# Attention's queries, keys and maxima as two float32r parts of 12 bits, in a 32-row tile for each head

## The reference

```python
def _L0_attn_ref(x, wq, bq, wk, bk, wv, bv, wo, bo):
    ...
    q = split(x @ wq.T + bq); k = split(x @ wk.T + bk); v = split(x @ wv.T + bv)
    scale = Dh ** 0.5
    scores = jnp.einsum('bhsd,bhtd->bhst', q, k) / scale
    scores = jnp.where(causal, scores, -jnp.inf)
    weights = jax.nn.softmax(scores, axis=-1)
    ctx = jnp.einsum('bhst,bhtd->bhsd', weights, v)
    return ctx.transpose(0, 2, 1, 3).reshape(B, S, E) @ wo.T + bo

x = x + 0.5 * _L0_ffn_ref(_layernorm(x), ...)     # 8 experts, top 2, capacity 1.25
x = x + _L0_attn_ref(_layernorm(x), ...)
x = x + 0.5 * _L0_ffn_ref(_layernorm(x), ...)
```

## Time and profile before

| | |
|---|---|
| median of 3 runs | 1033.29 us (1031.57 to 1038.26) |
| span of the profiled execution | 1036.6 us |
| PE busy | 831.8 us (80%) |
| DVE busy | 601.5 us (58%) |
| ACT busy | 523.4 us (50%) |
| POOL busy | 489.6 us (47%) |
| mean granted clock of PE | 0.890 |

### The profile page before, as it was taken

The page is one execution under the profiler, slowest core; times in us unless marked ns, Lnnn a source line. Parts: engine busy times, 40 slices in busy tenths (PEclk is TensorE's granted clock), DMA queues, the critical chain, the costliest instruction groups (busy, mean ns, idle before and its releaser), DMA issues. The chain is left out here.

```text
span 1036.6 us, 18080 instructions
## 1 busy us (share of the span) xinstructions
PE 831.8 (80%) x6599; PEld 446.5 (43%) x6599; DVE 601.5 (58%) x1237; ACT 523.4 (50%) x841; POOL 489.6 (47%) x686
## 2 busy tenths in 40 slices
PE   8569999944668988888978899878887618999990
PEld 7437878742212223332333323323232316787770
DVE  7931211124767788888787977878775423334235
ACT  6323343442237776777556786566766303433330
POOL 5047455325652662646467522562224651545453
PEclk9769999986657999999799999999899758999995
DMA  7115575621451262341524224323202124423236
GB/s 204 73 26 153 148 217 145 192 63 51 130 162 66 53 189 48 89 144 43 174 76 105 99 53 152 85 65 106 53 18 79 53 63 149 130 79 97 78 136 228
DMA packets 96185, 110.81 MB, mean 107 GB/s; under 512 B 12279, under 2 KB 68763, under 8 KB 96104
## 3 DMA queue, kind: packets, MB, share of 16 engines
q1 hardware_dynamic: 84752, 88.86, 29.1%
q0 software_dynamic: 9216, 17.98, 6.8%
q10 hardware_dynamic: 2136, 2.91, 0.8%
HBM read 57.86 MB, written 52.89 MB: 107 GB/s over the span
## 5 line engine op out<-in xcount | busy, mean ns | idle before, releaser
L1903 DVE TENSOR_REDUCE m_blk<-banks 128x8 f32<-128x1024 f32 (+1 forms) x320 | 348.5, 1114 | 79.7 <-PE banks L1505 67.1
L1823 ACT ACTIVATE pt<-banks 128x1024 f32<-128x1024 f32 (+3 forms) x384 | 300.4, 811 | 145.1 <-PE banks L1489 142.7
L1537 PE MATMUL banks<-pt,vs 128*32 128x512 f32 (+3 forms) x1536 | 176.6, 534 | 7.2 <-POOL pt L2252 3.8
L1489 PE MATMUL banks<-qb,kp 64*128 64x512 bf16 (+3 forms) x768 | 132.6, 351 | 53.7 <-DVE m_blk L1903 45.2
L2252 POOL TENSOR_SCALAR_AFFINE_SELECT pt<-pt 128x512 f32<-128x512 f32 x128 | 81.6, 637 | 192.1 <-ACT pt L1823 191.7
L1505 PE MATMUL banks<-kp,qa 64*128 64x128 bf16 (+4 forms) x1152 | 126.4, 294 | 19.6 <-ACT pt L1823 11.6
L849 POOL DMA_INDIRECT xe<-xn_rows,slot_tok x80 | 79.9, 999 | 94.4 <-PE banks L1190 37.2
L675 POOL DMA_INDIRECT y_tab<-ys,ids x70 | 68.0, 972 | 81.5 <-DVE ys L635 64.5
L1106 ACT ACTIVATE he<-banks,b_up 128x512 f32<-128x512 f32 (+1 forms) x96 | 57.9, 616 | 89.9 <-PE banks L1190 89.5
L1505 PEld LDWEIGHTS banks<-kp,qa 48*128 48x128 bf16 (+1 forms) x1152 | 46.2, 99 | 130.3 <-ACT pt L1823 92.7
L585 ACT ACTIVATE hT<-banks,bfc 128x512 f32<-128x512 f32 (+1 forms) x96 | 56.3, 615 | 84.9 <-DVE bfc L607 48.8
(11 more groups left out here) (344 smaller groups left out, 1128.8 us busy)
## 6 DMA issues: line engine op xcount, KB each, us to landing
bucket<-zero SPq DMA_DIRECT2D x16, 660.0 KB
qb<-q_stack SPq DMA_DIRECT2D x32, 192.0 KB, 3.5
qa<-q_stack SPq DMA_DIRECT2D x30, 192.0 KB, 3.3
kp<-k_stack SPq DMA_DIRECT2D x30, 192.0 KB, 4.2
q_stack<-qp SPq DMA_DIRECT2D x18, 256.0 KB
k_stack<-kq SPq DMA_DIRECT2D x18, 256.0 KB
y_slots<-ye SPq DMA_DIRECT2D x16, 256.0 KB, 2.5
mid<-x SPq DMA_DIRECT2D x8, 512.0 KB, 3.6
```

The costliest lines, as they stand in the source:

```text
L1489: i = nc.tensor.matmul(ring[SLOT["score", 2 * u + pair]][:, s, 0:w], kp[g][rows_s, pair, kb * P:(kb + 1) * P], qb[par][rows_s, pair, q0:q0 ...
L1537: i = nc.tensor.matmul(o_bank[VW * h:VW * h + VW, q:q + w], vs[par][:, kb, h, :], pt[u % PTS][:, h, 0:w], start=u in (0, SECOND), stop=u i ...
L1823: nc.scalar.activation(pt[u % PTS][:, 2 * pair:2 * pair + 2, 0:w], ring[SLOT["score", 2 * u + pair]][:, :, 0:w], ACT.Exp, scale=SCALE).the ...
L1903: nc.vector.tensor_reduce(dst, ring[slot][:, :, 0:blocks * P].rearrange("p s (j k) -> p s j k", k=P), AX.X, ALU.max).then_inc(m_done, 1)
```

## The change

Queries and keys become two float32r parts instead of three bf16 parts. float32r is a float32 whose writer rounds it to 12 bits of mantissa, so that a matmul takes it as a single operand; part 1 is what part 0 leaves. The products kept are part 0 by part 0, part 0 by part 1 and part 1 by part 0: three slots of 8 rows, 24 in all, plus 2 rows for the maximum and 4 for the diagonal. A head now has a tile of 32 rows, and the four heads of a group lie in the four quarters of the 128 partitions; `qa`, `qb` and `kp` lose the axis of pairs and hold 4 bytes per value, so their size is the same.

- `score` and `maxima`: as many matmuls of the same widths as before, on 32 rows (24 where the diagonal isn't marked) of float32r instead of 64 (48) of bf16. Pair 0 is in partitions 0 to 63, pair 1 in 64 to 127.
- ACT: `second_part` goes, 16 copies of 128x512; `stack_take` is 4 copies instead of 8. DVE and POOL: `third_part` goes (4 on DVE, 12 on POOL); DVE's `remainder` writes part 1 itself.
- POOL: `split_max` has 2 steps instead of 5, since the sign is now in `k_edge`. The constants take 20 selects on 32 rows in place of 10 on 64, and 6 copies in place of 12.
- PE in the prologue: `stack_parts` makes 12 matmuls instead of 32. The transpose of the maxima is float32 on 32 columns instead of bf16 on 48.
- DMA: three pieces for queries and three for keys in place of six and six, of the same total bytes; a load of a stack is four DMAs of 24 rows instead of two of 48 by 2; the maxima come back in four DMAs instead of two.

The diff, cut to its core:

```diff
-    Q_PART = [0, 0, 0, 1, 1, 2]
-    K_PART = [0, 1, 2, 0, 1, 0]
+    Q_PART = [0, 0, 1]
+    K_PART = [0, 1, 0]
+    HR = 32
     KS = len(Q_PART) * DH
     EDGE, STEP = KS + 4, 32
...
-            qa = [sba(f"qa{i}", [P, HS // 2, S], bf16) for i in range(2)]
-            qb = [sba(f"qb{i}", [P, HS // 2, S], bf16) for i in range(2)]
-            kp = [sba(f"kp{i}", [P, HS // 2, S], bf16) for i in range(NG)]
+            qa = [sba(f"qa{i}", [P, S], f32r) for i in range(2)]
+            qb = [sba(f"qb{i}", [P, S], f32r) for i in range(2)]
+            kp = [sba(f"kp{i}", [P, S], f32r) for i in range(NG)]
...
-            parts = [[sba(f"{n}{j}", [P, S], bf16) for j in range(3)] for n in ("qp", "kq")]
-            rest = sba("rest", [P, 2, 512])
+            parts = [[sba(f"{n}{j}", [P, S], f32r) for j in range(2)] for n in ("qp", "kq")]
...
-            m_neg = sba("m_neg", [P, HS, T // 2])
-            m_parts = [sba(f"m_parts{i}", [P, 3, HS, T // 2], bf16) for i in range(2)]
-            MR = 3 * HS * T // 2
-            m_rows = [sba(f"m_rows{i}", [MR, P], bf16) for i in range(2)]
+            m_parts = [sba(f"m_parts{i}", [P, 2, HS, T // 2], f32r) for i in range(2)]
+            MR = 2 * HS * T // 2
+            m_rows = [sba(f"m_rows{i}", [MR, P]) for i in range(2)]
...
-                for j in range(3):
-                    eng.wait_ge((part_one, rest_ok, split_ok)[j], 3 + which)
+                for j in range(2):
+                    if j == 0:
+                        eng.wait_ge(part_one, 3 + which)
+                    else:
+                        eng.wait_ge(c_evac, pro_at[("q1", "k1")[which]] + 1)
                     for c in range(len(order)):
                         if order[c] == j:
                             dst = stack[0:NH * KS, :].rearrange("(h c d) n -> c h d n", h=NH, d=DH)[c]
-                            eng.dma_start(dst[h0:h1], parts[which][j][h0 * DH:h1 * DH, :]).then_inc(done, 16)
+                            eng.dma_start(dst[h0:h1], parts[which][j][h0 * DH:h1 * DH, :].bitcast(f32)).then_inc(done, 16)
...
-                    src = stack[bass.ds(b * NH * KS + g * HS * KS, HS * KS), :].rearrange("(i s r) n -> s r i n", s=2, r=KS)
-                    for s in range(2):
-                        sp.dma_start(dst(s), src[s]).then_inc(done, 16)
+                    src = stack[bass.ds(b * NH * KS + g * HS * KS, HS * KS), :].rearrange("(h r) n -> h r n", r=KS)
+                    for h in range(HS):
+                        sp.dma_start(dst[HR * h:HR * h + KS, :].bitcast(f32), src[h]).then_inc(done, 16)
...
-                    for s in range(2):
-                        src = max_rows[hf * 3 * HS:(hf + 1) * 3 * HS, :].rearrange("(c i s) n -> s c i n", c=3, s=2)[s]
-                        dst = qb[par][64 * s + KS:64 * s + KS + 3]
-                        sp.dma_start(dst[:, :, hf * HALF:(hf + 1) * HALF], src).then_inc(max_ld[hf][par], 16)
+                    for h in range(HS):
+                        src = max_rows[hf * 2 * HS:(hf + 1) * 2 * HS, :].rearrange("(c h) n -> h c n", c=2)[h]
+                        dst = qb[par][HR * h + KS:HR * h + KS + 2, hf * HALF:(hf + 1) * HALF]
+                        sp.dma_start(dst.bitcast(f32), src).then_inc(max_ld[hf][par], 16)
...
                     kb = UNITS[u][1]
                     q0, w = unit_queries(u)
                     for s in range(2):
-                        rows_s = slice(64 * s, 64 * s + 64)
+                        h = 2 * pair + s
+                        rows_h = slice(HR * h, HR * h + HR)
                         i = nc.tensor.matmul(ring[SLOT["score", 2 * u + pair]][:, s, 0:w],
-                                             kp[g][rows_s, pair, kb * P:(kb + 1) * P],
-                                             qb[par][rows_s, pair, q0:q0 + w], start=True, stop=True)
+                                             kp[g][rows_h, kb * P:(kb + 1) * P],
+                                             qb[par][rows_h, q0:q0 + w], start=True, stop=True)
                     i.then_inc(s_full, 1)
...
-                            rows_s = slice(64 * s, 64 * s + (64 if diag else KS))
+                            h = 2 * pair + s
+                            rows_h = slice(HR * h, HR * h + (HR if diag else KS))
                             i = nc.tensor.matmul(ring[slot][:, s, at:at + blocks * P],
-                                                 qa[par][rows_s, pair, qt * P:(qt + 1) * P],
-                                                 kp[g][rows_s, pair, kb * P:(kb + blocks) * P],
+                                                 qa[par][rows_h, qt * P:(qt + 1) * P],
+                                                 kp[g][rows_h, kb * P:(kb + blocks) * P],
                                                  start=not diag or j == 0, stop=not diag)
...
-                    nc.tensor.transpose(m_bank[0:MR, 0:P], m_parts[turn_no][:].rearrange("p c h t -> p (c h t)"),
-                                        identb[:]).then_inc(c_full, 1)
+                    nc.tensor.transpose(c_bank[0:MR, 0:P],
+                                        m_parts[turn_no][:].bitcast(f32).rearrange("p c h t -> p (c h t)"),
+                                        ident[:]).then_inc(c_full, 1)
...
-                def stack_parts(half, which, j, pairs_of=range(PAIRS)):
-                    pe.wait_ge((part_one, rest_ok, split_ok)[j], 2 * half + which + 1)
+                def stack_parts(half, which, j):
+                    if j == 0:
+                        pe.wait_ge(part_one, 2 * half + which + 1)
+                    else:
+                        pe.wait_ge(c_evac, pro_at["qk"[which] + str(half)] + 1)
                     cols = slice(half * 512, half * 512 + 512)
-                    for i in pairs_of:
-                        to = ST_BANK[half][which][i]
-                        if j == 0:
-                            edge = (q_edge, k_edge)[which][:, None, :].broadcast_to([P, HB, P])
-                            nc.tensor.matmul(to.rearrange("p (t k) -> p t k", k=P), identb[:], edge, start=True, stop=False)
-                        m = nc.tensor.matmul(to, sel[:, which, j, i, :], parts[which][j][0:HS * DH, cols], start=False,
-                                             stop=j == 2)
-                        if j == 2:
-                            m.then_inc(st_full, 1)
+                    to = ST_BANK[half][which]
+                    if j == 0:
+                        edge = (q_edge, k_edge)[which][:, None, :].broadcast_to([P, HB, P])
+                        nc.tensor.matmul(to.rearrange("p (t k) -> p t k", k=P), identb[:], edge, start=True, stop=False)
+                    m = nc.tensor.matmul(to, sel[:, which, j, :], parts[which][j][0:HS * DH, cols], start=False,
+                                         stop=j == 1)
+                    if j == 1:
+                        m.then_inc(st_full, 1)
...
-                def second_part(use, which, half, slot):
-                    s = slice(half * 512, half * 512 + 512)
-                    act.wait_ge(c_evac, use + 1)
-                    nc.scalar.copy(parts[which][1][:, s], rest[:, slot, :]).then_inc(rest_ok, 1)
...
-                        if g == 1 and not bt.final and u in (6, 7, 8, 10):
-                            k = (6, 7, 8, 10).index(u)
-                            second_part(at[("q0", "q1", "k0", "k1")[k]], k // 2, k % 2, k % 2)
...
                 def stack_take(half, which):
-                    for i in range(PAIRS):
-                        act.wait_ge(st_full, 2 * PAIRS * half + PAIRS * which + i + 1)
-                        dst = (qa[0], kp[0])[which][:, i, half * 512:half * 512 + 512]
-                        nc.scalar.copy(dst, ST_BANK[half][which][i]).then_inc(st_evac, 1)
+                    act.wait_ge(st_full, 2 * half + which + 1)
+                    dst = (qa[0], kp[0])[which][:, half * 512:half * 512 + 512]
+                    nc.scalar.copy(dst, ST_BANK[half][which]).then_inc(st_evac, 1)
...
-                def third_part(which, half):
+                def remainder(use, b, which, half, src):
+                    k = 4 * b + (2 * half + which if b == 0 else 2 * which + half)
                     s = slice(half * 512, half * 512 + 512)
-                    dve.wait_ge(rest_ok, 2 * half + which + 1)
-                    nc.vector.tensor_tensor(parts[which][2][:, s], rest[:, which, :], parts[which][1][:, s],
-                                            ALU.subtract).then_inc(split_ok, 1)
-                def remainder(use, b, which, half, src):
-                    turn, slot = (2 * half + which, which) if b == 0 else (2 * which + half, half)
-                    k = 4 * b + turn
                     dve.wait_ge(part_one, k + 1)
-                    wait(dve, split_ok, k - 1)
-                    nc.vector.scalar_tensor_tensor(rest[:, slot, :], src, (bq_c, bk_c)[which][:],
-                                                   parts[which][0][:, half * 512:half * 512 + 512],
```

(27 more changed lines are left out.)

82 lines of the change are left out of this document (39 added, 43 removed).

## The result

The changed kernel takes 1191.15 us (median of 4, 1186.11 to 1210.86), the kernel before, run beside it, 1035.78 us: a ratio of 1.150, 95% interval 1.144 to 1.157. Medians are over all runs of a kernel; the ratios leave out its slow runs, those more than 1.5% above its fastest. The time lies 106 us above the range; the likeliest direction was right, the size was not. The profiled execution has a span of 1186.7 us in place of 1036.6, and its mean granted clock is 0.748 in place of 0.890. In these traces the granted clock stands at one of two levels, 1.00 (2.4 GHz) or 0.50 (1.2 GHz); a value between them is the mean of a stretch.

A forecast was written before the change was run, and what follows sets the result against it. It took a PE-DVE loop in attention's groups, no engine being full, as the bound. Gains -11.2, weights +5 and narrow matmuls +24 made +17.8 us: 1033.3 + 17.8 = 1051 us, term bounds 1040 to 1073, range 1016 to 1085.

The forecast's parts named there:

- (d): Attention: maxima and scores of different pairs stream together in rows of their own; -3.4 us, bounds 0 and -6.9.
- (a): First maxima: POOL's shorter split and an earlier chain of fetches cut PE's 4.67 us wait; -1.4 us, bounds -0.5 and -1.5.
- (b): SP's six stores in place of 12 before group 0's second-half maxima cut PE's 5.02 us wait; -3.5 us, bounds -1 and -5.
- (c): ACT's casts ahead of exponentials in group 1 of three batches go away; -2.9 us, bounds 0 and -7.3.
- (e): Constants: ten more selects are covered by POOL's wait of 33.08 us behind them; no cost.
- The gains together: Savings from prologue and attention, all gain terms: -11.2 us, bounds -1.5 and -20.7.
- Wide ones: 512-column float32r matmuls in attention stream at the bf16 rate, 0.23 us a pair; 0.43 us kept as the other end.
- rival of half rate: Attention's 4-byte columns stream at 0.43 us in place of 0.23, giving 1100 us; chance 0.15 for this or worse.
- two instructions: Each float32r matmul lowered to two, doubling their count: worse than 1100 us; shares the 0.15 chance of half rate or worse.
- Weights: Wide units: score of pair 1 starts with a slower weight load behind DVE's wait; +5 us, bounds 0 and +10.
- narrow: Diagonal maxima: eight matmuls with loads at the float32 rate, +0.57 us each, 1.6 us a group; +24 us, bounds 0 and +34.

The follow-up runs named there:

- e1: Kernel before, still bf16, scores and diagonal maxima over 32 rows in place of 64, other maxima 24 in place of 48: 1143.6 us, ratio 1.104.
- e2: Changed kernel, float32r kept, scores and diagonal maxima over 64 rows (two heads' summed), other maxima over 48: 1078.9 us, ratio 1.043 to the kernel before.
- e13: e5 with the diagonal maxima's mask rows moved to rows 52 to 55, so the other maxima leave them out: 1020.2 us, ratio 0.986 to the kernel before.
- e3: Changed kernel with bf16 in place of float32r, one 32-row tile per head and two parts kept: 1098.8 us, ratio 1.062 to the kernel before.
- e7: Kernel before, bf16, scores and diagonal maxima over all 128 rows, other maxima over 96: 1063.2 us, ratio 1.028.
- e5: Two bf16 parts in the 64-row layout of the kernel before, unused rows zero, prologue and stores as changed: 1021.2 us, ratio 0.988 to the kernel before.
- e8: e2 with the diagonal maxima's operands read as bf16, all else float32r: 1063.3 us, ratio 1.022 to the kernel before.
- e6: Changed kernel, float32r, scores and diagonal maxima over all 128 rows, other maxima over 96: 1113.6 us, ratio 1.077 to the kernel before.
- e12: e5 with scores and diagonal maxima over 32 rows, other maxima over 24, heads still starting at rows 0 and 64: 1139.9 us, ratio 1.102 to the kernel before.

## Why the prediction was wrong

**The step that failed** is one that the prediction never wrote down as a term: it read "PE's clock is at its upper level, 1.00" for the kernel before and took each duration at that level for the kernel after. The change from 64 to 32 rows stood in it only as a gain (d). No rival had the clock in it either, though a price was at hand: the pair of scores at 305.38 in the earlier trace rows takes 0.61 us and those in the earlier trace rows 0.39. What the runs showed in its place: over 32 rows attention ran at a clock of 0.67 (0.68 in bf16, e1), and 64 rows alone, the type kept, gave back 112 us (e2). That "slower" was the likeliest outcome was more than luck, since float32r costs 42 us in 64 rows too. The 155 us, by differences of medians: two parts alone -15 (e13 against before), float32r in 64 rows +59 (e2 against e13), from 64 to 32 rows in row groups of their own +112 (changed against e2). By the other way round, rows in bf16 +79 (e3 against e13), then the type +92. So the two losses are not independent, and no single number is the clock's share. The type costs more at the lower level: 0.38 us a wide unit (4.71 against 4.33 in e3), 0.21 at the upper. The stated bounds are a slip as well: the terms as given add up to 1013 to 1076 us, not 1040 to 1073.

**The terms, one by one.**
- (a) The split is two steps, 0.50 us from the first to the end of the last in place of 1.43, so the 0.9 us are there. PE's wait didn't shrink, 5.51 us in place of 4.67, because PE now comes to it earlier. From attention's first matmul to the transpose of the first maxima it is 33.6 us in place of 35.6 (35.6 in e1 and e7 too, 33.6 to 34.0 in all kernels made from the changed one), so the term is -1.6 to -2, a little beyond its bound of -1.5.
- (b) Six stores take 6.8 us to issue in place of 8.4, not half: with rows twice as long each took more. The four loads cost nothing extra, 1.11 us where two took 1.52. But the program then lets SP wait until the stores have landed, which the term had left out: SP's next issue, at 293.42, comes 5.0 us after the last store's, in place of 2.6. PE's wait went from 5.02 to 3.82 us, so -1.2 in place of -3.5, in one profile; over the other runs with the same float32r stores it lies between 0.96 and 5.78. In bf16 the stores take 3.85 us, and e5 and e13 show no such wait at all.
- (c) Of the two waits for an exponential in group 1 one of 0.17 us is left in that wide half of the changed kernel. In e13 the wide half of group 1 takes 22.55 us in place of 23.27, the same in each of three batches: -2.2 us, -2.9 forecast.
- (d) The overlap is real (starts 0.01 us apart in e3), but its 3.4 us at the upper level can't be singled out.
- (e) POOL still waits 29.98 us behind the constants in the changed kernel: the selects cost nothing.
- The gains together: -7.8 forecast for (a) to (c), which need neither the type nor the tiles; e13, which has them, shows 14.6 us less by medians, interval 11 to 17. More than forecast, then: (a) and (b), with the whole wait of 5.02 us gone, make some 7, and (c) 2; the rest is not traced.
- *Wide ones* at the bf16 rate: right, 0.24 us. The rival of half rate is out, and so are two instructions.
- *Weights* +5 and *narrow* +24: together 29. A plain group of e2 at the upper level takes 2.83 us more than before, an estimate of 42 us for 15. That is half as much again, and the make-up is another. A float32r load takes 204 ns on average in e2 (184 in the scores of that group), near the float32 one's 192. The Trainium skill, TensorE: Matmul & The Clock Gate, section Weight-path perf modes, has no fast load for FP32; it doesn't name float32r, but this number fits the same rule. The load shows behind every wait and between wide matmuls too, not only behind DVE's: the scores make 1.28 us a group, where 0.35 was forecast. The diagonal maximum costs 0.27 us more, not 0.57. The price of 0.57 came from float32 instructions, and the earlier trace rows says what they pay for: 128 columns take 0.112 us and 512 take 0.43, four times as much, so that time goes by columns and not by loads, and for columns the prediction itself took the bf16 rate. In a group the four cost 0.45 us (e8), not 1.6. The rest, 1.1 us, is by subtraction the other maxima, to which the prediction gave nothing; no run at 64 rows took their type away.
- The remaining 16 us or so of e2 against e13 stand beside a lower clock, 0.89 against 0.95. Why it is lower is open: over 128 rows float32r and bf16 both have 0.99 (e6, e7).

**Open too**: what of PE's work the granted clock answers to, beyond that rows do, that zeros count as well, and that scores and maxima add up to more than their single effects; and why the clock of e3 is above that of e12, 41 us. Float32r in 64 rows of which the rest are zero, the change's 24 bits without its fall of the clock, was not run: its proxy e2 suggests that it would lose to the kernel before.

## What to carry to other kernels

A row of a profile holds at the clock that it was taken at: where a change takes rows from PE's matmuls, put the lower level in as a rival, with its price from a row that shows it. Half the rows for the same columns saved no PE time here; filling a tile's unused rows with zeros cost no time and kept the clock (e5, e13), as long as two heads still had rows of their own to stream side by side. And an operation that sits off the end of a queue (the diagonal maxima) is priced by what waits behind it, not by its own length.

## What the runs showed of the hardware

- In these kernels the granted clock follows the rows that matmuls take: bf16 over 32 in place of 64 rows, the same instructions otherwise, 0.68 in place of 0.94 in attention (e1), 0.66 in place of 0.95 with zeros left out (e12, e5). PE was not idler for it: busy 92% of that stretch in e1 and 85% before, though at the lower level each matmul also lasts longer. Rows of zeros count: 0.95 with 26 to 30 rows of 64 filled.
- float32r streams 512 columns at bf16's pace (0.24 us from start to start), but its weight load takes 204 ns on average in e2, where bf16 has 95 before.
- Two heads' tiles of 64 rows overlap almost wholly: 0.23 us from pair to pair, 0.44 when each head takes all 128 rows (e7).
